# Attention stage of a two-layer block: two of ScalarE's four squares behind the next exponentials, VectorE's query remainder ahead of its wait for GpSimd, two row maxima ahead of x's statistics

## The chip, the cores and the metric

The kernel runs on one core of a Trainium2 chip. The metric is the device time of one launch in microseconds (us). TensorE does the matrix products into PSUM, VectorE (DVE in the rows) and ScalarE (ACT) read PSUM and SBUF, GpSimd (POOL) works from SBUF, and SyncE (SP) issues all DMAs of the stage that the change touches.

## What is computed

The reference has four steps for 32 sequences of 256 tokens with 256 features; the change lies in the first two and in the distances for the third:

```
def _layernorm(x):  m, v = mean(x), var(x);  return (x - m) / sqrt(v + eps)

x = x + tanh(g_xattn[0]) * xattn(_layernorm(x), ctx, ctx, wq, wk, wv, wo)   # 16 heads of 16
x = x + tanh(g_ffn[0])   * ffn(_layernorm(x), ...)
x = x + tanh(g_xattn[1]) * align(ctx, _layernorm(x))    # distances, path, gather
x = x + tanh(g_ffn[1])   * ffn_quantised(_layernorm(x), ...)

def xattn(query, key, value, ...):
    scores = q @ k.T / sqrt(256)                        # per head, 256 x 256
    return (softmax(scores) @ v) @ wo.T
def ffn(x, ...):
    h = bitlinear(x, w_fc) + gate * (x @ v.T @ fast_b.T @ u.T)    # 1024 wide
    r = maximum(h, 0)
    return bitlinear(r * r, w_proj)
```

## The kernel before

`build` calls three phases one after the other: `attention_phase` (line 103; the first two steps and the distances), `alignment_phase` and `last_layer_phase`. Only the first is changed.

`attention_phase` is a software pipeline over the 32 sequences ("batches", `NB`). Each engine runs a hand-written `iteration(i)`, for i from -4 to 33, in which several batches are at different stages: `a` = i+2 (queries and keys are made and split in three bf16 parts), `s` = i+1 (first scores and their row maxima), `i` (second scores, exponentials, values), `z` = i-1 (output projection, first half of the ffn), `y` = i-2 (second half of the ffn, distances), `nx` = i+3 (x's statistics). TensorE runs its iteration as a loop, the others unrolled. The order on each engine is the order of the calls in `iteration`; between engines only semaphores hold things together (`w(name, count)` waits, `.then_inc` counts up). An engine works strictly in its order: what stands behind a waiting instruction waits too.

The pieces that matter here, with their lines:

- **Scores, first pass.** `scores1` (L380) writes the scores of head h into the PSUM tile `s1[h % 2]`; `maxima` on VectorE (L799) reduces it to negative row maxima `nmax`. With two tiles, scores of head h+2 wait for the maxima of head h. After head 15 `max_transpose` (L387) turns `nmax`, and `split_max` (L739, L740) makes two bf16 rows of it, which a DMA puts under the queries.
- **Scores, second pass.** `scores2` (L395) writes `s2[h % 2]`, `exps` on ScalarE (L595) takes the exponentials into `pt[h % 8]`, `values` (L407) multiplies four heads at a time. Scores of head h+2 wait for the exponential of head h; `values(g)` waits for exponentials up to head 4g+3.
- **The ffn's squares.** `fc(z, k)` (L473 to L477), k = 0 to 3, makes 256 of the 1024 columns; `relu` (L625, ScalarE) makes `rl[k % 2]` from it with two instructions and, in the kernel before, the high half of its square at once, `r2h` (L631). GpSimd squares `rl` exactly into the only buffer `r2` (L886), and `low_squares` on VectorE (L768) makes the low half `r2l` from `r2` and `r2h`. GpSimd's next square waits for it. `proj` (L344, L345) uses both halves in the next iteration.
- **The norms.** VectorE collects statistics (`x_stats`, and inside `residual1`, `residual2`; L713), aggregates them (L719), writes the variances `ln_v` (L832) and waits for `ln_rstd`: GpSimd raises them to the power -0.5 (L897, `ln_y`). Then VectorE makes `yn` (`ln3`), `xh2` (`ln2`) and `xhat` (`ln1`), all on L725.
- **The query remainder.** `queries` (L321) fills the bank `B_QUERIES`; `qh_copy` (L574, ScalarE) rounds it to `qp`, `q_remainder` (L749, VectorE) makes `qr` from bank and copy. `turn_xh2` (L315), which transposes `xh2` into the same bank (`B_XH2`; three PSUM tiles `wb` serve 18 uses in turn), waits for `ln2` and for `q_remainder`:

```
def turn_xh2(b):
    w("ln2", b.n + 1)
    w("qh_cp", b.n + 4), w("q_rem", b.n + 4)
```

- **The key remainder** (L745, `kr`) opens VectorE's iteration, in the same way as the query's.

In the rows buffer numbers are left out: `s` is s1 or s2 (L380 writes s1, L395 s2), `pt` the exponentials, `wb` the shared PSUM banks, `xh` is xh2, `x` is x1 or x2, and `r` is r2.

Of the kernel before, what the change touches and what calls it, by code (L numbers as in the profile page):

```python
# [102 lines left out]
def attention_phase(nc, io, scr):  # L103
# [3 lines left out]
    with ExitStack() as ctx:  # L107
# [84 lines left out]
        def unrolled(iteration):  # L192
            for n in range(-4, NB + 2):
                iteration(Batch(n // 2, n % 2))
# [20 lines left out]
        def there(b):  # L215
            return not isinstance(b.n, int) or 0 <= b.n < NB
# [342 lines left out]
        @block.scalar  # L559
        def _(act):  # L560
            def w(s, count, most=NB):
                done(act, e[s] if isinstance(s, str) else s, count, most)

            def xT_copy(b):
                w("xhat_t", b.n + 1), w("q_mm", b.n)
                act.activation(xT[:], B_TURN_X[:], ACT.Copy).then_inc(e["xT_cp"], 1)

            def kh_copy(b):
                w("k_mm", b.n + 1), w("k_out", 16 * b.n, 16 * NB)
                act.activation(kp[:, 0, :, :], B_KEYS[:], ACT.Copy).then_inc(e["kh_cp"], 1)  # L570

            def qh_copy(b):
                w("q_mm", b.n + 1), w("q_out", 16 * b.n, 16 * NB)
                act.activation(qp[:, 0, :, :], B_QUERIES[:], ACT.Copy, scale=1.0 / 16).then_inc(e["qh_cp"], 1)  # L574

            def middle_part(b, rem, r, parts, s):
                w(rem, b.n + 1)
                act.activation(parts[:, 1, :, :], r[:], ACT.Copy).then_inc(e[s], 1)

            def onT_copy(b):  # L580
                w("on_t", b.n + 1), w("wo_mm", b.n)
                act.activation(onT[:], B_TURN_ON[:], ACT.Copy).then_inc(e["onT_cp"], 1)

            def values_copy(b):
                w("v_mm", b.n + 1), w("av_mm", NG * (b.n - 1), NG * NB)
                for t in range(T):
                    last = act.activation(vw[b.p][:, t, :, 0:DH], B_VALUES[:, t, :].rearrange("p (h m) -> p h m", m=DH),
                                          ACT.Copy)
                last.then_inc(e["vw_cp"], 1)

            def exps(b, lo, hi):
                for h in range(lo, hi):
                    w("s2_mm", NH * b.n + h + 1, NH * NB)
                    w("av_mm", NG * b.n + h // HPG - 1, NG * NB)
                    act.activation(pt[h % (2 * HPG)][:], s2[h % 2][:], ACT.Exp).then_inc(e["expd"], 1)  # L595

            def copy_group(b, g):
                w("av_mm", NG * b.n + g + 1, NG * NB)
                w("o_t", 2 * (b.n - 1) + g // 2 + 1, 2 * NB)
                act.activation(osb[:, g, :], oacc[:, g % 2, :], ACT.Copy).then_inc(e["o_cp"], 1)  # L600

            def yT_copy(b):
                w("y_t", b.n + 1), w("ab_mm", b.n)
                act.activation(yT[:], B_TURN_Y[:], ACT.Copy).then_inc(e["yT_cp"], 1)

            def xh2_copy(b):
                w("xh2_t", b.n + 1), w("fc_mm", 4 * b.n, 4 * NB)
                act.activation(x2h[:], B_XH2[:], ACT.Copy).then_inc(e["x2T_cp"], 1)

            def low_copy(b):  # L610
                w("low_mm", b.n + 1), w("fc_mm", 4 * b.n, 4 * NB)
                act.activation(lowt[:], B_LOW[:, 1, :], ACT.Copy).then_inc(e["low_cp"], 1)

            def half_copy(b):
                w("half_t", b.n + 1), w("ab_mm", b.n)
                for t in range(T):
                    rows = slice(32 * t, 32 * t + 32)
                    last = act.activation(hrows[rows, t * P:t * P + P], B_LOW[rows, 0, 0:P], ACT.Copy)
                last.then_inc(e["half_cp"], 1)

            def relu(b, k):
                w("fc_mm", 4 * b.n + k + 1, 4 * NB)
                w("squared", 4 * b.n + k - 1, 4 * NB)
                for j in range(2):
                    last = act.activation(rl[:, k % 2, j, :], B_FC[k][:, j, :], ACT.Relu,  # L625
                                          scale=fscl[:, 2 * k + j:2 * k + j + 1])
                last.then_inc(e["relu"], 1)
                w("relu", 4 * b.n + k + 1, 4 * NB)
                if k == 0:
                    w("pr_mm", b.n)  # L630
                act.activation(r2h[:, 2 * k:2 * k + 2, :], rl[:, k % 2], ACT.Square).then_inc(e["sq_high"], 1)  # L631

            def ctx_squares(b):
                w(c_in[b.p], 16 * (b.half + 1), 16 * NB)
                w("dist", b.n - 1)
                for t in range(T):
                    w("aa_sum", T * b.n + t, T * NB)
                    act.activation(junk[:], cin[b.p][:, t, :], ACT.Square, accum_out=aa[b.p][:, t:t + 1])\
                        .then_inc(e["aa_sum"], 1)

            def distance(b):
                w("ab_mm", b.n + 1), w("d_out", 16 * T * b.n, 16 * T * NB)
                w("aa_sum", T * (b.n + 1), T * NB)
                for t in range(T):
                    last = act.activation(dd[:, t, :], B_PRODUCTS[:, t, :], ACT.Relu, bias=aa[b.p][:, t:t + 1], scale=-2.0)  # L645
                last.then_inc(e["dist"], 1)

            def iteration(i):
                s, a, z, y = i.off(1), i.off(2), i.off(-1), i.off(-2)
                if there(a):  # L650
                    xT_copy(a)
                    kh_copy(a)
                if there(z):
                    onT_copy(z)
                if there(a):
                    middle_part(a, "k_rem", kr, kp, "k_parts_mid")
                if there(z):
                    ctx_squares(z)
                if there(i):
                    exps(i, 0, 4)  # L660
                if there(a):
                    qh_copy(a)
                if there(i):
                    copy_group(i, 0)
                    exps(i, 4, 6)
                if there(s):
                    values_copy(s)
                if there(i):
                    exps(i, 6, 8)
                if there(y):  # L670
                    yT_copy(y)
                if there(z):
                    xh2_copy(z)
                if there(a):
                    middle_part(a, "q_rem", qr, qp, "q_parts_mid")
                if there(y):
                    half_copy(y)
                if there(i):
                    copy_group(i, 1)
                if there(y):  # L680
                    distance(y)
                if there(z):
                    low_copy(z)
                if there(i):
                    exps(i, 8, 10)
                if there(z):
                    relu(z, 0)
                if there(i):
                    exps(i, 10, 12)
                if there(z):  # L690
                    relu(z, 1)
                if there(i):
                    exps(i, 12, 14)
                    copy_group(i, 2)
                    exps(i, 14, 16)
                if there(z):
                    relu(z, 2)
                if there(i):
                    copy_group(i, 3)
                if there(z):  # L700
                    relu(z, 3)
            unrolled(iteration)

        @block.vector
        def _(v):
# [106 lines left out]
            def iteration(i):  # L812
                s, a, nx, z, y = i.off(1), i.off(2), i.off(3), i.off(-1), i.off(-2)
                if there(a):
                    k_remainder(a)
                if there(nx):
                    x_stats(nx)
                if there(s):
                    maxima(s, 0, 4)
                if there(y):  # L820
                    residual2(y)
                if there(s):
# [4 lines left out]
                if slots:  # L827
                    w("halves", y.n)
                    aggregate(slots[0], slots[-1] + 1)
                    c = slice(T * slots[0], T * (slots[-1] + 1))  # L830
                    w("ln_rstd", i.n + 3, NB + 5)
                    v.tensor_scalar(ln_v[:, c], ln_mv[:, c, 1], EPS, None, ALU.add).then_inc(e["ln_var"], 1)  # L832
                    w("ln_rstd", i.n + 4, NB + 5)
                if there(y):
                    ln3(y)
                if there(z):
                    ln2(z)
                if there(a):
                    q_remainder(a)
                if there(nx):  # L840
                    ln1(nx)
                if there(z):
# [1001 lines left out]
```

## Time and profile before

| | |
|---|---|
| median of 3 runs | 1934.49 us (1932.57 to 1935.65) |
| profiled execution | 1930.39 us, its span 1928.6 us |
| TensorE busy, of the span | 1454.7 us (75%) |
| VectorE busy | 1438.4 us (75%) |
| ScalarE busy | 1108.1 us (57%) |
| GpSimd busy | 560.7 us (29%) |

The span is drawn from the first to the last instruction; the time of the run holds about 2 us more. Busy shares are means over three phases. The attention phase ends a little after 1230 us; what the tables say of it is read from windows inside it. A row of the timeline has the start, the duration of the merged group, the engine, the line, the operation, the tiles (written <- read), the count, and in brackets the idle time before it and whom it waited for.

### The profile page before, as it was taken

What the parts mean: (1) busy time and instruction counts of PE and PEld (TensorE: products, weight loads), DVE (VectorE), ACT (ScalarE), POOL (GpSimd) and SP (SyncE); (2) the same over time, 40 slices, a digit from 0 to 9 for tenths busy, and PEclk for the clock granted to TensorE, in tenths of its full rate; (3) what the DMA queues carried; (4) which work ended last, traced back from release to release, by engine and by line L of the source; (5) the groups of instructions that cost most, each with busy time, mean ns of one, the idle gap of its engine ahead of it and who ended that gap; (6) DMA issues with size and microseconds to landing.
All of it is one profiled execution on the core that took longest, in us unless ns stands there. A gap on an engine that the chain in (4) does not pass through costs nothing. (4 is left out here: it accounts for less than half of the span.)

```text
span 1928.6 us, 35799 instructions
## 1 busy us (share of the span) xinstructions
PE 1454.7 (75%) x10821; PEld 1062.1 (55%) x10821; DVE 1438.4 (75%) x4102; ACT 1108.1 (57%) x2374; POOL 560.7 (29%) x1002
## 2 busy tenths in 40 slices
PE   1689999999999999999999997423333001889986
PEld 1367777777777777777777775300000000566664
DVE  7466667666666676666666664299999998999996
ACT  0166666666666666666666665224333300899997
POOL 4112222322222222222222222210000000778786
PEclk9799999999999999999999999755555555899999
DMA  2544444434444344344443421222221001232221
GB/s 74 123 140 111 130 113 140 117 106 133 118 120 121 109 140 119 106 131 118 125 118 109 128 76 39 58 64 61 58 59 28 0 0 49 66 99 91 91 89 45
DMA packets 322936, 179.49 MB, mean 93 GB/s; under 512 B 93793, under 2 KB 318193, under 8 KB 322802
## 3 DMA queue, kind: packets, MB, share of 16 engines
q1 hardware_dynamic: 322802, 178.07, 33.5%
q8 instruction: 40, 0.66, 0.1%
q14 instruction: 94, 0.77, 0.1%
HBM read 122.91 MB, written 50.33 MB: 90 GB/s over the span
## 5 line engine op out<-in xcount | busy, mean ns | idle before, releaser
L799 DVE TENSOR_REDUCE nmax<-s 128x2 f32<-128x512 f32 x512 | 325.1, 682 | 41.1 <-PE s L380 40.0
L595 ACT ACTIVATE pt<-s 128x512 f32<-128x512 f32 x512 | 277.4, 596 | 83.7 <-PE s L395 83.6
L886 POOL TENSOR_TENSOR r<-rl 128x512 f32<-128x512 f32 x128 | 133.3, 1042 | 369.4 <-ACT rl L625 366.8
L380 PE MATMUL s<-kst,qst 96*128 96x256 bf16 x1024 | 163.3, 276 | 18.2 <-DVE nmax L799 12.8
L395 PE MATMUL s<-qst,kst 128*128 128x256 bf16 x1024 | 167.6, 276 | 9.2 <-ACT pt L595 1.4
L1298 PE MATMUL gate<-diag,one 128*128 128x512 f16 x35 | 21.3, 608 | 176.7 <-DVE left L1385 176.7
L625 ACT ACTIVATE rl<-wb,fscl 128x256 f32<-128x256 f32 x256 | 107.4, 473 | 81.1 <-PE wb L477 81.1
L473 PE MATMUL wb<-x2l,wfcT 128*128 128x256 f32 x512 | 143.3, 302 | 0.5 <-ACT dd L645 0.5
L407 PE MATMUL oacc<-pt,vw 128*32 128x256 f32 x2048 | 137.1, 385 | 2.0 <-ACT pt L595 2.0
L344 PE MATMUL wb<-wprT,r2l 128*128 128x256 f32 x512 | 129.3, 292 | 6.9 <-DVE r2l L768 6.9
L474 PE MATMUL wb<-x2h,wfcT 128*128 128x256 f32 x512 | 132.7, 281 | 0.0
L897 POOL TENSOR_TENSOR ln_y<-ln_v,ln_pow 128x6 f32<-128x6 f32 (+2 forms) x37 | 44.6, 1204 | 298.7 <-DVE ln_v L832 298.6
L1408 DVE SCALAR_TENSOR_TENSOR hop<-iota,path,steps 32x256 f32<-32x256 f32 x255 | 120.7, 473 | 12.4 <-DMA steps<-step 3.4
L345 PE MATMUL wb<-wprT,r2h 128*128 128x256 f32 x512 | 123.6, 281 | 0.0
L768 DVE TENSOR_TENSOR r2l<-r,r2h 128x512 fp32r<-128x512 f32 x128 | 88.3, 690 | 45.7 <-POOL r L886 45.7
L395 PEld LDWEIGHTS s<-qst,kst 128*128 128x128 bf16 x1024 | 81.0, 98 | 73.3 <-ACT pt L595 48.6
L380 PEld LDWEIGHTS s<-kst,qst 96*128 96x128 bf16 x1024 | 91.4, 98 | 53.3 <-DVE nmax L799 31.7
L1298 PEld LDWEIGHTS gate<-diag,one 128*128 128x128 f16 x35 | 3.7, 105 | 194.1 <-DVE left L1385 175.5
L344 PEld LDWEIGHTS wb<-wprT,r2l 128*128 128x128 f32 x512 | 97.2, 190 | 8.6 <-DVE r2l L768 7.9
L1372 DVE TENSOR_TENSOR_SCAN rows_r<-best,rows_r,rows_d 128x64 f32<-128x64 f32 x280 | 100.7, 360 | 0.2
L1584 ACT ACTIVATE apart<-iota,mid 128x256 f32<-128x256 f32 x64 | 28.7, 509 | 124.0 <-DVEq L1790 118.9
L473 PEld LDWEIGHTS wb<-x2l,wfcT 128*128 128x128 f32 x512 | 97.0, 189 | 2.0 <-issue 0.6
(266 smaller groups left out, 3963.3 us busy)
## 6 DMA issues: line engine op xcount, KB each, us to landing
kst<-k_parts_dram SPq DMA_DIRECT2D x384, 64.0 KB, 2.7
qst<-q_parts_dram SPq DMA_DIRECT2D x384, 64.0 KB, 2.4
k_parts_dram<-kp SPq DMA_DIRECT2D x32, 384.0 KB, 5.1
q_parts_dram<-qp SPq DMA_DIRECT2D x32, 384.0 KB, 3.1
xin<-in_x_dram SPq DMA_DIRECT2D x32, 256.0 KB, 2.9
cT<-in_ctx_T_dram SPq DMA_DIRECT2D x32, 256.0 KB, 2.7
xres<-in_x_dram SPq DMA_DIRECT2D x32, 256.0 KB, 3.2
cin<-in_ctx_dram SPq DMA_DIRECT2D x32, 256.0 KB, 4.4
```

The source lines that it names most:

```text
L344: pe.matmul(B_PROJ[:, t, :], r2l[:, f, t * P:t * P + P], wprT[:, f, :], start=(f == 0), stop=False)
L345: last = pe.matmul(B_PROJ[:, t, :], r2h[:, f, t * P:t * P + P], wprT[:, f, :], start=False, stop=(f == FT - 1))
L380: last = pe.matmul(s1[h % 2][:, t, :], qst[b.p][0:MAXROW, h, t * P:t * P + P], kst[b.p][0:MAXROW, h, :], start=True, stop=True)
L395: last = pe.matmul(s2[h % 2][:, t, :], kst[b.p][:, h, t * P:t * P + P], qst[b.p][:, h, :], start=True, stop=True)
L407: last = pe.matmul(oacc[HW * j:HW * j + HW, g % 2, :], vw[b.p][:, t, HPG * g + j, :], pt[(HPG * g + j) % (2 * HPG)][:, t, :], start=(t == ...
L473: pe.matmul(B_FC[k][:, j, :], wfcT[:, c, f * P:f * P + P], x2l[:, c, :], start=(c == 0), stop=False)
L474: pe.matmul(B_FC[k][:, j, :], wfcT[:, c, f * P:f * P + P], x2h[:, c, :], start=False, stop=False)
L595: act.activation(pt[h % (2 * HPG)][:], s2[h % 2][:], ACT.Exp).then_inc(e["expd"], 1)
L625: last = act.activation(rl[:, k % 2, j, :], B_FC[k][:, j, :], ACT.Relu, scale=fscl[:, 2 * k + j:2 * k + j + 1])
L799: v.tensor_reduce(nmax[:, T * h:T * h + T], s1[h % 2][:], AX.X, ALU.max, negate=True)\
L886: pool.tensor_tensor(r2[:], rl[:, k % 2], rl[:, k % 2], ALU.mult)\
L1408: ch.link(v.scalar_tensor_tensor(hop[:], iota[:], path[:, i + 1:i + 2], steps[:, i, :], ALU.is_le, ALU.mult, accum_out=path[:, i:i + 1]))
```

## The change

ScalarE: the square leaves `relu` and becomes a function `square` of its own, called for k = 0 after `exps(i, 10, 12)` and for k = 1 after `exps(i, 12, 14)`; for k = 2 and 3 it still follows its `relu`. VectorE: `maxima(s, 0, 2)` is called ahead of `x_stats(nx)`, and `q_remainder(a)` ahead of the wait for `ln_rstd` and thus ahead of `ln3` and `ln2`. No instruction is added or removed.

```
                     last = act.activation(rl[:, k % 2, j, :], B_FC[k][:, j, :], ACT.Relu,
                                           scale=fscl[:, 2 * k + j:2 * k + j + 1])
                 last.then_inc(e["relu"], 1)
+
+            def square(b, k):
                 w("relu", 4 * b.n + k + 1, 4 * NB)
                 if k == 0:
                     w("pr_mm", b.n)
...
                 if there(i):
                     exps(i, 10, 12)
                 if there(z):
+                    square(z, 0)
                     relu(z, 1)
                 if there(i):
                     exps(i, 12, 14)
+                if there(z):
+                    square(z, 1)
+                if there(i):
                     copy_group(i, 2)
                     exps(i, 14, 16)
                 if there(z):
                     relu(z, 2)
+                    square(z, 2)
                 if there(i):
                     copy_group(i, 3)
                 if there(z):
                     relu(z, 3)
+                    square(z, 3)
...
                 if there(a):
                     k_remainder(a)
+                if there(s):
+                    maxima(s, 0, 2)
                 if there(nx):
                     x_stats(nx)
                 if there(s):
-                    maxima(s, 0, 4)
+                    maxima(s, 2, 4)
...
                     w("ln_rstd", i.n + 3, NB + 5)
                     v.tensor_scalar(ln_v[:, c], ln_mv[:, c, 1], EPS, None, ALU.add).then_inc(e["ln_var"], 1)
+                if there(a):
+                    q_remainder(a)
+                if slots:
                     w("ln_rstd", i.n + 4, NB + 5)
                 if there(y):
                     ln3(y)
                 if there(z):
                     ln2(z)
-                if there(a):
-                    q_remainder(a)
                 if there(nx):
                     ln1(nx)
```

On ScalarE, in a steady iteration from the ffn's first quarter to its third, there stood before (`s2_0`, `s2_1` are the two tiles of second scores, `rl` and `r2h` the relu and its square):

```order
L625 ACTIVATE rl<-wb0,fscl 128x256 x2
L631 ACTIVATE r2h<-rl 128x512
L595 ACTIVATE pt2<-s2_0 128x512
L595 ACTIVATE pt3<-s2_1 128x512
L625 ACTIVATE rl<-wb1,fscl 128x256 x2
L631 ACTIVATE r2h<-rl 128x512
L595 ACTIVATE pt4<-s2_0 128x512
L595 ACTIVATE pt5<-s2_1 128x512
L600 ACTIVATE osb<-oacc 128x256
```

and now stands, with the lines of the changed kernel (2 higher from L631 on):

```order
L625 ACTIVATE rl<-wb0,fscl 128x256 x2
L595 ACTIVATE pt2<-s2_0 128x512
L595 ACTIVATE pt3<-s2_1 128x512
L633 ACTIVATE r2h<-rl 128x512
L625 ACTIVATE rl<-wb1,fscl 128x256 x2
L595 ACTIVATE pt4<-s2_0 128x512
L595 ACTIVATE pt5<-s2_1 128x512
L633 ACTIVATE r2h<-rl 128x512
L600 ACTIVATE osb<-oacc 128x256
```

Each square went behind the two exponentials that followed it.

On VectorE, at the start of a steady iteration, there stood before (`xin0` is x's tile for the statistics, `s1_0` and `s1_1` the tiles of first scores):

```order
L745 TENSOR_TENSOR kr<-wb1,kp 128x512
L713 BN_STATS ln_st<-xin0 128x6 x2
L799 TENSOR_REDUCE nmax<-s1_0 128x2
L799 TENSOR_REDUCE nmax<-s1_1 128x2
L799 TENSOR_REDUCE nmax<-s1_0 128x2
```

and now:

```order
L753 TENSOR_TENSOR kr<-wb1,kp 128x512
L807 TENSOR_REDUCE nmax<-s1_0 128x2
L807 TENSOR_REDUCE nmax<-s1_1 128x2
L721 BN_STATS ln_st<-xin0 128x6 x2
L807 TENSOR_REDUCE nmax<-s1_0 128x2
```

The two reductions for heads 0 and 1 went ahead of the two statistics instructions.

On VectorE, around the wait for GpSimd's power (behind `ln_v`), there stood before:

```order
L832 TENSOR_SCALAR ln_v<-ln_mv 128x6
L725 TENSOR_SCALAR yn<-x2,ln_mv,ln_y 128x256 x2
L725 TENSOR_SCALAR xh2<-x1_0,ln_mv,ln_y 128x256 x2
L749 SCALAR_TENSOR_TENSOR qr<-wb2,qp 128x512
L725 TENSOR_SCALAR xhat<-xin0,ln_mv,ln_y 128x256 x2
```

and now:

```order
L842 TENSOR_SCALAR ln_v<-ln_mv 128x6
L757 SCALAR_TENSOR_TENSOR qr<-wb2,qp 128x512
L733 TENSOR_SCALAR yn<-x2,ln_mv,ln_y 128x256 x2
L733 TENSOR_SCALAR xh2<-x1_0,ln_mv,ln_y 128x256 x2
L733 TENSOR_SCALAR xhat<-xin0,ln_mv,ln_y 128x256 x2
```

The query remainder went from behind `xh2` to ahead of `yn` and of the wait that stands in front of it.

## Rows read from the trace of the kernel before

**Rows 1.** Busy time by window, steady attention: us, busy (count) per engine, PEclk, DMA share, GB/s

```profile
180.00:1127.00 947.00, 923.33 (x7372) 718.53 (x7371) 648.63 (x1428) 618.98 (x1381) 257.02 (x379) 1.00 0.43 120
```

**Rows 2.** Timeline of TensorE, first scores of heads 2 and 3, iterations 21 and 29

```profile
818.56 0.27 PE L345 MATMUL wb<-wprT,r2h 128*128 128x256 f32 x1
818.81 0.39 PE L380 MATMUL s<-kst,qst 96*128 96x256 bf16 x2
819.41 0.39 PE L380 MATMUL s<-kst,qst 96*128 96x256 bf16 x2 [0.20 <-DVE nmax L799]
...
1098.97 0.61 PE L380 MATMUL s<-kst,qst 96*128 96x256 bf16 x4
```

**Rows 3.** Timeline of VectorE, iteration 21, its start

```profile
817.42 0.75 DVE L713 BATCH_NORM_STATS2 ln_st<-xin 128x6 f32<-128x256 f32 x2
818.08 2.47 DVE L799 TENSOR_REDUCE nmax<-s 128x2 f32<-128x512 f32 x4
```

**Rows 4.** Timeline of TensorE, turns of yn and xh2 and the values behind them, iterations 21 and 29

```profile
830.45 0.60 PE L315 MATMUL wb<-ident,yn 128*128 128x128 f32 x4
831.41 0.63 PE L315 MATMUL wb<-ident,xh 128*128 128x128 f32 x4 [0.36 <-DVE qr L749]
831.97 1.07 PE L407 MATMUL oacc<-pt,vw 128*32 128x256 f32 x16
...
1110.24 0.60 PE L315 MATMUL wb<-ident,yn 128*128 128x128 f32 x4
...
1111.36 1.07 PE L407 MATMUL oacc<-pt,vw 128*32 128x256 f32 x16
```

**Rows 5.** Timeline of VectorE, iteration 21, norms and query remainder

```profile
829.28 0.73 DVE L725 TENSOR_SCALAR yn<-x,ln_mv,ln_y 128x256 f32<-128x256 f32 x2 [1.45 <-POOL ln_y L897]
829.93 0.73 DVE L725 TENSOR_SCALAR xh<-x,ln_mv,ln_y 128x256 f32<-128x256 f32 x2
830.58 0.69 DVE L749 SCALAR_TENSOR_TENSOR qr<-wb,qp 128x512 f32<-128x512 f32 x1
```

**Rows 6.** Timeline of GpSimd, the power; one small step in iterations 21 and 32

```profile
827.92 1.33 POOL L897 TENSOR_TENSOR ln_y<-ln_v,ln_pow 128x6 f32<-128x6 f32 x1 [8.51 <-DVE ln_v L832]
...
831.05 0.20 POOL L905 TENSOR_TENSOR hrest<-half,hpb 128x2 f32<-128x2 f32 x1
...
1204.89 0.20 POOL L905 TENSOR_TENSOR hrest<-half,hpb 128x2 f32<-128x2 f32 x1
```

**Rows 7.** Timeline of ScalarE, iteration 21: the query copy, exponentials of heads 6 and 7

```profile
826.50 0.60 ACT L574 ACTIVATE qp<-wb 128x512 bf16<-128x512 f32 x1 [2.59 <-PE wb L321]
...
830.43 1.08 ACT L595 ACTIVATE pt<-s 128x512 f32<-128x512 f32 x2
```

**Rows 8.** Timeline of TensorE, iterations 20 and 21: second scores of heads 12 to 15, and behind

```profile
805.90 0.88 PE L395 MATMUL s<-qst,kst 128*128 128x256 bf16 x4
...
840.90 0.88 PE L395 MATMUL s<-qst,kst 128*128 128x256 bf16 x4
...
843.26 0.88 PE L395 MATMUL s<-qst,kst 128*128 128x256 bf16 x4
843.98 0.60 PE L380 MATMUL s<-kst,qst 96*128 96x256 bf16 x4
...
846.70 0.28 PE L387 MATMUL wb<-ident,nmax 128*32 128x128 f32 x1
```

**Rows 9.** Timeline of ScalarE, iteration 21: squares and exponentials of heads 10 to 13

```profile
839.73 0.63 ACT L631 ACTIVATE r2h<-rl 128x512 fp32r<-128x512 f32 x1
840.27 1.06 ACT L595 ACTIVATE pt<-s 128x512 f32<-128x512 f32 x2
841.22 0.84 ACT L625 ACTIVATE rl<-wb,fscl 128x256 f32<-128x256 f32 x2
...
842.63 1.06 ACT L595 ACTIVATE pt<-s 128x512 f32<-128x512 f32 x2
```

**Rows 10.** Timeline of VectorE, iteration 21: maxima of heads 14 and 15

```profile
844.40 1.29 DVE L799 TENSOR_REDUCE nmax<-s 128x2 f32<-128x512 f32 x2 [0.48 <-PE s L380]
```

More of the change, by code:

```diff
@@ L627, in relu, with square @@
                 last.then_inc(e["relu"], 1)
+            def square(b, k):
                 w("relu", 4 * b.n + k + 1, 4 * NB)
@@ L690, in iteration @@
                 if there(z):
+                    square(z, 0)
                     relu(z, 1)
@@ L693, in iteration @@
                     exps(i, 12, 14)
+                if there(z):
+                    square(z, 1)
+                if there(i):
                     copy_group(i, 2)
@@ L697, in iteration @@
                     relu(z, 2)
+                    square(z, 2)
                 if there(i):
@@ L701, in iteration @@
                     relu(z, 3)
+                    square(z, 3)
             unrolled(iteration)
@@ L815, in iteration @@
                     k_remainder(a)
+                if there(s):
+                    maxima(s, 0, 2)
                 if there(nx):
@@ L818, in iteration @@
                 if there(s):
-                    maxima(s, 0, 4)
+                    maxima(s, 2, 4)
                 if there(y):
@@ L832, in iteration @@
                     v.tensor_scalar(ln_v[:, c], ln_mv[:, c, 1], EPS, None, ALU.add).then_inc(e["ln_var"], 1)
+                if there(a):
+                    q_remainder(a)
+                if slots:
                     w("ln_rstd", i.n + 4, NB + 5)
@@ L837, in iteration @@
                     ln2(z)
-                if there(a):
-                    q_remainder(a)
                 if there(nx):
```

## The prediction

> **What bounds the kernel now.** I read the slices and the busy time by window first. In the steady stretch of the attention phase TensorE is busy 923.33 of 947 us at a granted clock of 1.00, which is its level of 2.4 GHz, while VectorE and ScalarE are busy two thirds of it [rows 1]. TensorE sets the pace there, so an edit on another engine is worth what it takes from TensorE's waits. Then I read the waits and TensorE's timeline of one period. The period is 35.00 us (the same group of second scores starts at 805.90 and 840.90, [rows 8]) and repeats unchanged from iteration 2 to 28. All rows here are from iteration 21 (813.4 to 848.4 us) or from iteration 29, which lacks x's statistics. The chain that ended last lies in the third phase and says nothing about this one. Three places in the period have TensorE waiting for work that the change moves:
>
> - *First scores of heads 2 and 3.* The last projection matmul starts at 818.56, and its kind comes 0.12 apart, so the scores could start near 818.68. They start at 818.81, and the second pair only at 819.41: four matmuls take from 818.81 to 819.80, 0.99 us, where iteration 29 shows 0.61 [rows 2]. The wait is for the maxima, which VectorE starts at 818.08, behind x's statistics [rows 3]. In iteration 29, without these statistics, it is gone.
> - *The turn of xh2.* It starts at 831.41 for want of the query remainder, 830.58 + 0.69 = 831.27 [rows 4, 5].
> - *Second scores of heads 12 to 15.* Both groups of four take 0.88 us [rows 8] where an undisturbed one takes 0.61 (the same count and columns, [rows 2]): their second pair waits for an exponential.
>
> **The change part by part.**
>
> *A, squares behind exponentials.* Before, a square starts at 839.73 and the exponentials of heads 10, 11 at 840.27: it holds them back by 0.54 us [rows 9]. Now they start at 839.73, then the square, and the relu for k = 1 starts at 841.22 as before, since the same work stands ahead of it. It lasts until the next instruction at 841.22 + 0.87 = 842.09 (0.84 and the step to the next), and the exponentials of heads 12, 13 start there, not at 842.63: 0.54 earlier. Scores of head 15 wait for the exponential of head 13. It ended at 842.63 + 1.06 = 843.69 and the following first scores started at 843.98 [rows 8, 9]; now it ends at 843.15 and these start at about 843.45. I take 0.53 us per iteration. The first group's stall (0.27 and the start) lies inside this: TensorE comes earlier to the second group and meets the rest there, about 0.3 us of waiting that stays. What the later squares cost: the copy of the values' third group keeps its time, since the second square still stands ahead of it. VectorE's low half for k = 0 waits for a square that ends near 841.3, for k = 1 near 843.7, about 0.9 us later than before. VectorE works in order and the maxima of heads 14, 15 stand behind; they would start near 844.35 and end near 845.64, against 844.40 and 845.69 before [rows 10]. The transpose of the maxima, at 846.70 before [rows 8], comes at 846.17. So 0.5 us of cover is left; if it were gone, each further microsecond would be TensorE's. GpSimd's second square waits for the low half of k = 0 (near 842.05) and for the relu (842.06): nothing. It applies in iterations 1 to 31, in which exponentials and squares meet: 31 x 0.53 = 16.4 us.
>
> *B, the query remainder under the power.* VectorE sits 1.45 us in front of yn for the power, which GpSimd runs from 827.92 to 829.25 [rows 5, 6]. The remainder needs ScalarE's copy, done at 827.10 [rows 7]; it starts at about 827.83 and ends at 828.5, inside this wait. Its cost is nothing; uncovered it would be 0.60 (its step to the next) in front of yn and xh2. xh2 is ready at 829.93 + 0.73 = 830.66 and TensorE, four matmuls behind 830.45 (0.60 for the group, the last of them 0.27 long and 0.11 apart, so 0.44 to the next), comes for it at 830.89. So the stall of 0.52 goes. What is late next: the values of heads 4 to 7 wait for the exponential of head 7, which ends at 830.43 + 1.08 = 831.51 [rows 7]. They start at 831.56, not at 831.97: 0.41 us. Iteration 29 has a power that is 0.3 shorter and no xhat, and shows this limit: from the turn of yn to the values 1.12 us, against 1.52 here [rows 4], a gain of 0.40. I take 0.41 and iterations 1 to 28: 11.5 us. GpSimd's second part of the queries and their DMA keep their place behind ScalarE's middle part, which does not move.
>
> *C, two maxima ahead of x's statistics.* The maxima of heads 0, 1 start at 817.42 and end at 818.10 and 818.70; TensorE wants them at 818.68 and 818.91, so both parts of the stall go: 0.13 + 0.38 = 0.51 at most, I take 0.49. The statistics and heads 2, 3 then end at about 820.6 as before, and VectorE still waits for TensorE behind them. Nobody waits for the statistics before the aggregate. Iterations 2 to 28: 27 x 0.49 = 13.2 us. In iterations before that the maxima stand in one unbroken row on VectorE, whose end doesn't move: nothing.
>
> No DMA is moved and no wait on SyncE's queue gains a later event than before; its transfers are issued from events that move forward with TensorE.
>
> *Where a page and the sum differ.* TensorE's idle time by the window row is 947 - 923.33 = 23.7 us in 27 periods, 0.87 us each [rows 1], and A, B and C together claim 1.43. The two can both hold because a row's duration covers a matmul's way through the array, so that short waits between matmuls hide inside durations; I count from start to start. The Trainium skill says just this in "Perfetto Trace Analysis", section Identifying the Most-Contended Engine: matmul busy share is no good measure of the room left, the share of weight loads is better. Here weight loads are busy 718.53 of 947 us, 76% [rows 1], which leaves far more room than 0.87 us. By the busy rows alone the sum would be that of the second rival.
>
> *Sum.* 16.4 + 11.5 + 13.2 = 41.1 us. The profiled execution has 1930.39 (span 1928.6); 1930.39 - 41.1 = 1889.3. The median of the runs shown lies 4.1 us above the profiled one, so the forecast against it is **1893.4 us**, 2.1% below 1934.49. The later phases keep their time.
>
> **Rivals.**
>
> 1. *The remainder slows the power.* GpSimd's power and VectorE's remainder now run together, and if one held the other up by the remainder's 0.69 us, yn would end at 830.70 and xh2 at 831.35, and TensorE would be at 831.49, 0.08 later than before. B would turn from 11.5 saved to 2 lost: 1893.4 + 13.7 = 1907. Against: a small GpSimd step right beside the remainder took 0.20 us, and 0.20 too where VectorE was idle [rows 6]. For: the power itself never ran beside it. Chance 0.11.
> 2. *Only visible idle time comes back.* The bracketed idle is 0.20 for C and 0.36 for B [rows 2, 4] and none for A: 0.56 x 28 = 16 us, so 1918. Against: the 0.88 and 0.61 us groups and iteration 29. Chance 0.06.
> 3. *Slower: the squares hold up VectorE.* The two low halves now wait for later squares with four reductions queued behind. From the point where the maxima of head 15 end after 846.1 TensorE waits at their transpose, and from about 2 us of delay, 1.43 + 0.5, the change loses. With 3 us it is about 1 us in each of 31 iterations: 1934.5 + 31 = 1966. For: the margin is small beside this chain of four engines. Against: every link is reckoned from rows, with 0.5 left. Chance 0.04.
> 4. *Nothing.* The moved work is on the path nowhere, because another wait takes each place (the relu of k = 3, a DMA): 1934. The order of the instructions does move as the change says. Chance 0.03.
>
> **How the numbers follow.** The forecast has 0.76. Its bounds: per iteration from 0.40 + 0.32 + 0.38 = 1.10 to 0.54 + 0.41 + 0.51 = 1.46, and up to 4 us at the pipeline's ends and between runs: 1887 to 1904. To hold 8 in 10 with some of rival 1, the range is 1886 to 1909. A measurement here tells a change of about 0.2% (4 us) from none; faster by more are the forecast and rivals 1 and 2, 0.93; the same 0.03; slower 0.04.
>
> **What would show it.** Right: a period of about 33.6 us instead of 35.0; no wait of the xh2 turn for qr; first scores of heads 2, 3 in one group of 0.61; the second scores of heads 12, 13 at 0.61 and those of 14, 15 still stretched; the power still 1.33 us; the values of heads 4 to 7 directly behind the exponential of head 7. Wrong: the transpose of the maxima waiting for VectorE, a power near 2 us, or a new wait of TensorE that isn't in the list of before.

## The result, and the profile after

| | before | changed |
|---|---|---|
| median (4 runs each, same chip) | 1933.53 us (1931.96 to 1935.65) | 1883.97 us (1883.32 to 1887.86) |
| profiled execution | 1930.39 us | 1887.86 us, its span 1886.1 us |
| ratio, 95% interval | | 0.9752 (0.974 to 0.9763) |
| steady period of the attention phase | 35.00 us | 33.40 us |

Faster by 2.5%, where 2.1% were forecast: 1883.97 against 1893.4, and 2 us below the lower end of the range. Two later sets of runs of the changed kernel gave medians of 1887.63 and 1886.46 us, ratios 0.9764 (0.9747 to 0.978) and 0.9761 (0.9748 to 0.9774). Both medians lie just inside the range, so the first is on the favourable side of what the kernel does. But the gain from median to median was 49.6 us at first and 46.9 and 46.3 later, against 41.1 forecast: most of the miss stays.

Busy time by window of the changed kernel's steady stretch (columns as in [rows 1]):

```profile
180.00:1080.00 900.00, 894.57 (x7329) 722.50 (x7331) 646.40 (x1423) 606.51 (x1374) 253.04 (x378) 1.00 0.45 126
```

The granted clock is 1.00 as before. TensorE's rows leave 5.4 of 900 us idle, 0.20 us a period, against 0.87: the rows show 0.67 us of a gain that is 1.60 by the starts. Counting from start to start was right.

The timeline of TensorE in the changed kernel, the three places in order of the iteration (the period that begins near 815 us):

```profile
820.59 0.61 PE L380 MATMUL s<-kst,qst 96*128 96x256 bf16 x4
821.04 0.60 PE L395 MATMUL s<-qst,kst 128*128 128x256 bf16 x4
...
831.86 0.60 PE L315 MATMUL wb<-ident,yn 128*128 128x128 f32 x4
832.30 0.60 PE L315 MATMUL wb<-ident,xh 128*128 128x128 f32 x4
833.06 1.07 PE L407 MATMUL oacc<-pt,vw 128*32 128x256 f32 x16 [0.16 <-ACT pt L595]
```

The first scores of heads 2 and 3 are one group of 0.61 us, where there were 0.99 in two [rows 2]. The turn of xh2 waits for nothing, but the values of heads 4 to 7 now wait for an exponential: from the turn of yn to these values 1.20 us, against 1.52 [rows 4].

And one period earlier, its last third:

```profile
806.35 0.61 PE L395 MATMUL s<-qst,kst 128*128 128x256 bf16 x4
...
808.41 0.61 PE L395 MATMUL s<-qst,kst 128*128 128x256 bf16 x4
...
810.40 0.63 PE L395 MATMUL s<-qst,kst 128*128 128x256 bf16 x4
810.87 0.60 PE L380 MATMUL s<-kst,qst 96*128 96x256 bf16 x4
...
813.60 0.28 PE L387 MATMUL wb<-ident,nmax 128*32 128x128 f32 x1
```

Both groups that took 0.88 [rows 8] take 0.61 and 0.63. The stretched rest in the second group, which the forecast left, isn't there. From the group for heads 10, 11 to the transpose of the maxima it is 7.25 us; before it was 8.04 (838.66 to 846.70, the first of these from the same timeline).

The timeline of ScalarE there:

```profile
806.54 0.84 ACT L625 ACTIVATE rl<-wb,fscl 128x256 f32<-128x256 f32 x2 [1.09 <-PE wb L477]
807.27 1.09 ACT L595 ACTIVATE pt<-s 128x512 f32<-128x512 f32 x2
808.23 0.65 ACT L633 ACTIVATE r2h<-rl 128x512 fp32r<-128x512 f32 x1
808.75 0.86 ACT L625 ACTIVATE rl<-wb,fscl 128x256 f32<-128x256 f32 x2
809.46 1.12 ACT L595 ACTIVATE pt<-s 128x512 f32<-128x512 f32 x2
```

The exponentials start 0.73 and 0.71 us after the relus in front of them. The square started 0.87 after its relu before: the forecast carried that 0.87 over to the exponentials. An exponential starts before the relus have ended (807.27 against 806.54 + 0.84 = 807.38), a square that follows its relus only after their end (839.73 against 838.86 + 0.84 = 839.70). From the kernel before, the relus ahead of the first square in [rows 9]:

```profile
838.86 0.84 ACT L625 ACTIVATE rl<-wb,fscl 128x256 f32<-128x256 f32 x2 [1.08 <-PE wb L477]
```

From relu to relu it is 2.21 us, where it was 2.36 (838.86 to 841.22). The square is not slow to start by itself: behind the two exponentials it starts 0.96 us after their start, and the relu that stood there before started after 0.95 (840.27 to 841.22, [rows 9]).

On VectorE and GpSimd:

```profile
811.20 0.69 DVE L776 TENSOR_TENSOR r2l<-r,r2h 128x512 fp32r<-128x512 f32 x1 [0.35 <-ACT r2h L633]
811.81 1.28 DVE L807 TENSOR_REDUCE nmax<-s 128x2 f32<-128x512 f32 x2
813.92 0.28 DVE L747 CAST nsp<-wb 32x128 bf16<-32x128 f32 x1 [0.83 <-PE wb L387]
```

```profile
829.19 0.69 DVE L757 SCALAR_TENSOR_TENSOR qr<-wb,qp 128x512 f32<-128x512 f32 x1
```

```profile
829.33 1.33 POOL L908 TENSOR_TENSOR ln_y<-ln_v,ln_pow 128x6 f32<-128x6 f32 x1 [8.01 <-DVE ln_v L842]
```

The low half does wait for the late square, and the last maxima end at 813.09, 0.51 us ahead of their transpose on TensorE: the cover of rival 3 was 0.5 as reckoned. The power takes 1.33 us with the remainder beside it, as before [rows 6]: rival 1 is out.

### The profile page after: what moved, and what is told of

The parts are those of the page before. It is cut to its first block and busy times, and to the rows that moved or that the text cites. A ratio compares the mean times of both kernels' runs of the same rounds, so it can differ in the third digit from the quotient of the medians.

```text
span 1886.1 us, 35769 instructions
## 1 busy us (share of the span) xinstructions
PE 1433.6 (76%) x10790; PEld 1074.4 (57%) x10821; DVE 1436.9 (76%) x4102; ACT 1097.6 (58%) x2374; POOL 558.5 (30%) x1002
## 5 line engine op out<-in xcount | busy, mean ns | idle before, releaser
L595 ACT ACTIVATE pt<-s 128x512 f32<-128x512 f32 x512 | 281.4, 612 | 70.0 <-PE s L395 70.0
L380 PE MATMUL s<-kst,qst 96*128 96x256 bf16 x1024 | 158.9, 275 | 11.8 <-DVE nmax L807 7.3
L395 PE MATMUL s<-qst,kst 128*128 128x256 bf16 x1024 | 157.3, 275 | 1.1 <-ACT pt L595 0.8
L345 PEld LDWEIGHTS wb<-wprT,r2h 128*128 128x128 f32 x512 | 99.2, 194 | 0.0
```

The source lines that it names most:

```text
L345: last = pe.matmul(B_PROJ[:, t, :], r2h[:, f, t * P:t * P + P], wprT[:, f, :], start=False, stop=(f == FT - 1))
L380: last = pe.matmul(s1[h % 2][:, t, :], qst[b.p][0:MAXROW, h, t * P:t * P + P], kst[b.p][0:MAXROW, h, :], start=True, stop=True)
L395: last = pe.matmul(s2[h % 2][:, t, :], kst[b.p][:, h, t * P:t * P + P], qst[b.p][:, h, :], start=True, stop=True)
```

## The experiments

Theory D: the surplus is in part A. A square that follows its relu directly reads what the relu has just written and waits for its end; an exponential doesn't. Each square moved frees this wait, some 0.14 us, besides its own 0.54. Rival R: A is worth the 0.53 of the forecast, and the rest arises from the parts together. A second question is where the spread of several us between executions comes from, since the sum was shifted by 4.1 us for it. Theory T: it lies in TensorE's clock in the last iterations.

**Each part alone.** The edits are the hunks of the change: ScalarE's alone, the one with `q_remainder` alone, the one with `maxima` alone.

> Only part A (the squares of k = 0 and 1 behind the next exponentials). Theory D (a square reads what the relu just wrote and must wait for its end, an exponential need not; each moved square frees 0.54 us and about 0.14 of that wait besides): period 34.21 us instead of 35.00, relu to exponential 0.73 us instead of relu to square 0.87, both groups of second scores of heads 12 to 15 at 0.61 to 0.63; time lower by 31 x 0.79 = 24 us. Rival R (A is worth the 0.53 of the forecast and the rest of the surplus comes from the parts together): period 34.47, the second group still stretched, 16 us.

> Only part B (query remainder ahead of the wait for the power). If the stage in the changed kernel tells its worth (turn of yn to values of heads 4 to 7 1.52 to 1.20 us): period 34.68, time lower by 28 x 0.32 = 9 us. By the forecast's 0.41: period 34.59, 11.5 us. The power stays at 1.33 us in both.

> Only part C (two maxima ahead of x's statistics). Both theories: period 34.49 us, time lower by 27 x 0.51 = 14 us; if parts interact (a sum larger than its parts) the three single gains per period add to clearly less than 1.60 us.

| | period | less than 35.00 by | median (runs) | ratio, 95% interval |
|---|---|---|---|---|
| A alone | 34.19 us | 0.81 | 1908.46 (4) | 0.9868 (0.9851 to 0.9884) |
| B alone | 34.68 us | 0.32 | 1926.36 (5) | 0.9965 (0.9951 to 0.9979) |
| C alone | 34.50 us | 0.50 | 1919.29 (4) | 0.9923 (0.9906 to 0.994) |
| all three | 33.40 us | 1.60 | see above | |

Kernel before in these runs: 1934.49 us. The single gains add to 1.63, all three together give 1.60: the parts are independent to 0.03 us, and R is out. A is worth 0.81 and not 0.53; C is what was forecast; B is worth 0.32 and not 0.41. TensorE and ScalarE in the kernel with B alone and in the changed kernel show the same rest, here from B alone:

```profile
822.21 0.60 PE L315 MATMUL wb<-ident,yn 128*128 128x128 f32 x4
822.65 0.60 PE L315 MATMUL wb<-ident,xh 128*128 128x128 f32 x4
823.41 1.07 PE L407 MATMUL oacc<-pt,vw 128*32 128x256 f32 x16 [0.16 <-ACT pt L595]
```

In the changed kernel the exponentials of heads 6 and 7:

```profile
831.84 1.09 ACT L595 ACTIVATE pt<-s 128x512 f32<-128x512 f32 x2
```

They end at 832.93 and the values start at 833.06: 0.13 us from the end of what is waited for to the matmul, where I had put 0.05.

The 0.05 came from iteration 29 of the kernel before, and it is right for that iteration. TensorE's iteration is a loop only from 4 to 27 (`run`); the iterations ahead of it and behind it are written out. The changed kernel shows both. In iteration 28, outside the loop, ScalarE, then TensorE's turns, then its weight loads (PEld):

```profile
1032.28 1.09 ACT L595 ACTIVATE pt<-s 128x512 f32<-128x512 f32 x2
1032.30 0.60 PE L315 MATMUL wb<-ident,yn 128*128 128x128 f32 x4
1033.42 0.59 PEld L407 LDWEIGHTS oacc<-pt,vw 128*32 128x32 f32 x16 [0.32 <-ACT pt L595]
```

The exponentials end at 1033.37 and the values' first weight load starts at 1033.42, 0.05 later, although it has waited. From the turn of yn it is 1.12 us, as in iteration 29 of before. The single instructions of the trace show what differs: outside the loop the weight load carries the wait for the exponential itself; inside it a register instruction of 0.03 us carries it, 0.08 ahead of the weight load. So it is in every trace of a kernel with B: 0.12 us to the weight load in the loop's iterations, 0.05 outside. With B alone the period is 34.61 outside the loop and 34.68 inside.

**One square at a time.** The first edit keeps the square of k = 1 behind its relu, the second that of k = 0:

```
                 if there(z):
                     square(z, 0)
                     relu(z, 1)
+                    square(z, 1)
                 if there(i):
                     exps(i, 12, 14)
-                if there(z):
-                    square(z, 1)
```

```
                 if there(z):
                     relu(z, 0)
+                    square(z, 0)
                 if there(i):
                     exps(i, 10, 12)
                 if there(z):
-                    square(z, 0)
                     relu(z, 1)
```

Both without B and C.

> Only the square of k = 0 moved; that of k = 1 stays behind its relu. The exponentials of heads 10, 11 come early, then square and relu as before, so by the forecast's reckoning the relu of k = 1 starts when it did and the second scores of head 15 too: period 35.00 us, nothing gained. Theory D (a square that follows its relu directly waits about 0.14 us for its end): relu to relu is 2.21 us instead of 2.36, the exponentials of heads 12, 13 come 0.15 earlier, period 34.85.

> Only the square of k = 1 moved. The stall of the group for heads 12, 13 stays (0.88), that of heads 14, 15 goes: 0.27 and 0.1 in front of it, period near 34.6 us by both theories. They differ in the step from the relu of k = 1 to the exponential: 0.87 us by the forecast, 0.73 by theory D.

The first has a period of 34.86 us. Theory D said 34.85, the forecast's reckoning 35.00. ScalarE in it:

```profile
837.32 0.84 ACT L625 ACTIVATE rl<-wb,fscl 128x256 f32<-128x256 f32 x2 [1.08 <-PE wb L477]
838.05 1.09 ACT L595 ACTIVATE pt<-s 128x512 f32<-128x512 f32 x2
839.00 0.65 ACT L633 ACTIVATE r2h<-rl 128x512 fp32r<-128x512 f32 x1
839.52 0.86 ACT L625 ACTIVATE rl<-wb,fscl 128x256 f32<-128x256 f32 x2
840.41 0.63 ACT L633 ACTIVATE r2h<-rl 128x512 fp32r<-128x512 f32 x1
```

One trace has both steps: relu to exponential 0.73 us, relu to square 0.89, and relu to relu 2.20 with the same three instructions in it that took 2.36 in the other order. The median was 1931.21 us (8 runs), 0.9992 (0.9982 to 1.0002) of before: by time alone this 0.14 us a period, 4 us in all, wouldn't be seen; the period shows it.

The second has 34.62 us, a gain of 0.38, near 34.6 as both theories said, with 0.88 in the first group and 0.61 in the second, and a step of 0.71 from the relu of k = 1 to the exponential. Its ratio is 0.9945 (0.9925 to 0.9966), from 2 runs. So the squares are worth 0.14 and 0.38 one by one and 0.81 together. The first square's 0.54 reaches TensorE only if the second lets it: moved alone, the exponentials of heads 12, 13 hold the second group (TensorE waits 0.35 in front of it and it takes 0.88):

```profile
841.58 0.88 PE L395 MATMUL s<-qst,kst 128*128 128x256 bf16 x4 [0.35 <-ACT pt L595]
```

What counts is not a sum of two terms but the later of two waits.

**The spread between executions.**

> The changed kernel unchanged, for the spread of its executions. Theory T (the place of a profiled execution in its kernel's spread differs by some us with TensorE's clock in the last four iterations, whose waits are long): period 33.40 again to 0.02 us, iterations 31 to 33 between 87 and 93 us in sum, shorter where the granted clock is higher, and the time follows them. Rival: the steady period varies between executions and carries the spread.

> The kernel before unchanged, for a second trace of it. Theory T (the profiled execution of before had a high granted clock in its last iterations and so stood below its median): the last three periods add to more than the 87.5 us of that one, the time is nearer 1934 than 1930, the steady period is 35.00 again.

In both kernels the steady periods repeat to a few hundredths (35.00 and 33.40 in every trace, the latter 33.33 outside TensorE's loop; the kernel before has 35.25 twice, in iterations 10 and 26, in both of its traces). What differs is the phase's end. Iterations 31 to 33, from the half norms' transpose of iteration 30 to that of 33, as windows of the four traces: kernel before (profiled 1930.39 us), kernel before again (1934.73), changed kernel (1887.86), changed kernel again (1883.92):

```profile
1144.98:1232.52 87.54, 65.28 (x486) 50.46 (x483) 36.35 (x82) 42.25 (x97) 19.59 (x36) 0.95 0.12 31
```

```profile
1144.97:1236.48 91.51, 69.30 (x486) 53.43 (x483) 36.34 (x82) 42.24 (x97) 19.55 (x36) 0.88 0.11 30
```

```profile
1099.62:1191.34 91.72, 70.18 (x486) 54.35 (x483) 36.28 (x82) 41.70 (x97) 19.56 (x36) 0.86 0.11 30
```

```profile
1098.81:1187.12 88.31, 66.74 (x486) 52.01 (x483) 36.30 (x82) 41.69 (x97) 19.59 (x36) 0.90 0.12 31
```

The counts are the same; the length follows the granted clock (0.95 and 0.90 against 0.88 and 0.86), and the differences of 4.0 and 3.4 us are nearly those of the times, 4.3 and 3.9. They stand in TensorE's own busy time, 65.28 against 69.30 and 66.74 against 70.18 for the same matmuls, while the other engines' hardly differs. Theory T holds. Here TensorE waits for other engines and falls to its level of 1.2 GHz in stretches that differ from one execution to the next; in the changed kernel's profiled execution such a stretch shows by the step of the matmuls:

```profile
1149.03 0.28 PE L344 MATMUL wb<-wprT,r2l 128*128 128x256 f32 x1
...
1150.34 0.41 PE L344 MATMUL wb<-wprT,r2l 128*128 128x256 f32 x1
1150.56 0.41 PE L345 MATMUL wb<-wprT,r2h 128*128 128x256 f32 x1
```

They come 0.22 us apart instead of 0.12. The profiled execution of before had an end with a high clock and stood low in its spread, that of the changed kernel one with a low clock and stood high.

**Going on from there.** After the change TensorE still stood at two places: the key projection waited about 0.2 us for the relu of k = 3 of the iteration before (they share a PSUM tile), and the values of heads 4 to 7 for the exponential of head 7. The first edit, on TensorE and VectorE:

```
                 if there(a):
                     turn_x(a)
-                    keys(a)
-                if there(z):
-                    turn_on(z)
                 if there(s):
                     scores1(s, 0, 2)
+                if there(a):
+                    keys(a)
+                if there(z):
+                    turn_on(z)
...
-                if there(a):
-                    k_remainder(a)
                 if there(s):
                     maxima(s, 0, 2)
+                if there(a):
+                    k_remainder(a)
```

> The changed kernel, with TensorE's first scores of heads 0, 1 ahead of the key projection and VectorE's maxima 0, 1 ahead of the key remainder. The key projection waits about 0.2 us for the relu of k = 3 (same PSUM tile); the scores would cover it. If nothing else waits for the keys: period 33.40 - 0.2 = 33.2 us, 6 us less than the changed kernel. Rival: the key remainder comes 0.3 later on VectorE, ScalarE's and GpSimd's key parts follow, and the maxima of heads 2, 3 behind it hold the scores of heads 4, 5: period 33.4 or more.

The period is 33.06 us, 0.34 less, and the ratio to before 0.9739 (0.9722 to 0.9756) at a median of 1881.07 us (5 runs). I had expected 0.2. TensorE in it:

```profile
812.41 0.60 PE L315 MATMUL wb<-ident,xhat 128*128 128x128 f32 x4
812.85 0.60 PE L380 MATMUL s<-kst,qst 96*128 96x256 bf16 x4
813.28 1.89 PE L321 MATMUL wb<-cT,wkT 128*128 128x256 f32 x8
815.01 0.60 PE L315 MATMUL wb<-ident,on 128*128 128x128 f32 x4
```

in the changed kernel:

```profile
815.35 0.60 PE L315 MATMUL wb<-ident,xhat 128*128 128x128 f32 x4
816.01 1.99 PE L321 MATMUL wb<-cT,wkT 128*128 128x256 f32 x8
817.84 0.60 PE L315 MATMUL wb<-ident,on 128*128 128x128 f32 x4
```

The wait of 0.22 is gone, and 0.10 within the projection besides: it takes 1.73 us from its start to the next group where it took 1.83 behind the wait. By the single matmuls the 0.10 lies between the first and the second (0.32 us against 0.22). Why was not tried apart.

The second edit exchanges TensorE's calls for heads 6 and 7, alone and with the first:

```
                 if there(s):
                     values_proj(s)
-                    scores1(s, 6, 8)
                 if there(i):
                     scores2(i, 6, 8)
+                if there(s):
+                    scores1(s, 6, 8)
```

> The changed kernel with only the exchange of scores for heads 6, 7: period 33.40 - 0.1 = 33.30 us if the exponential of head 6 starts 0.1 earlier, 33.40 if not; 3 us at most.

> Keys behind the first scores as in the run before, and TensorE's second scores of heads 6, 7 ahead of the first scores of heads 6, 7. What B left over is the wait of the values of heads 4 to 7 for the exponential of head 7 (0.32 us a period). The exponential of head 6 starts at the end of ScalarE's values copy, 0.1 later than an instruction that waits for nothing could, because its scores are just ready; 0.44 us earlier scores give this 0.1 back: period 33.06 - 0.1 = 32.96 us, 3 us less. If the values copy is the limit to the last, 33.06.

> The changed kernel unchanged, on the same chip as the two others: period 33.40 us, time 1883 to 1889 us, following the granted clock in the last four iterations.

| five runs each, same chip | period | median | ratio to before, 95% interval |
|---|---|---|---|
| changed kernel | 33.40 us | 1886.46 us | 0.9761 (0.9748 to 0.9774) |
| heads 6, 7 exchanged | 33.26 us | 1882.81 us | 0.9749 (0.9736 to 0.9763) |
| both edits | 32.95 us | 1878.60 us | 0.9720 (0.9707 to 0.9733) |

The kernel before had 1932.8 us (9 runs). The exchange gives 0.14 of the period alone (0.1 was expected) and 0.11 behind the other edit; by time alone it can't be told from the changed kernel, as the intervals overlap. The exponentials of heads 6, 7 start 0.54 us behind ScalarE's copy of the values, where it was 0.66: that is the 0.1. The version with both beats the changed kernel: the intervals of the two ratios don't touch.

## Why the prediction was wrong

The direction and the three places were as forecast, and the rivals fell. The range was missed by 2 us, by one term, and in part by a first set of runs on the fast side.

- **A, the term that was mis-sized.** The step that failed is "Now they start at 839.73, then the square, and the relu for k = 1 starts at 841.22 as before, since the same work stands ahead of it". The same instructions did stand there, but not the same waits. The exponentials start 0.73 us behind the relu, not 0.87, and the relu of k = 1 starts 2.21 behind the first, not 2.36. A gives 0.79 to 0.81 a period, not 0.53; over 31 periods 8 us more. In all the exponentials of heads 12, 13 come 0.85 us earlier behind the first relu (2.92 us, before 3.77), 0.54 of the moved square and 0.15 and 0.16 of its waits. That is enough for TensorE's two groups to be whole again, so "about 0.3 us of waiting that stays" fell too. The term's upper bound, 0.54, left no room for this.
- **B.** The limit was named rightly, the exponential of head 7; the release took 0.13 us and not 0.05 in the 24 iterations of TensorE's loop. The gain there is 0.32 and not 0.41, over 24 periods 2.2 us less; outside the loop it is 0.40 and more, as forecast. Iteration 29, which I took for proof of 0.40, is written out behind the loop: the step was read from code that differs from the steady one.
- **C.** 0.50 to 0.51 against 0.49, as forecast.
- **The sum.** By the corrected terms 31 x 0.80 + 24 x 0.32 + 4 x 0.41 + 27 x 0.51 = 47.9 us, of which 47.1 up to the last transpose of the maxima, in iteration 30. Measured there are 46.2 (1158.74 against 1112.55) in the first traces of both kernels and 46.95 in the second ones. The three parts together give 1.60 and not 1.63, 0.8 less in 27 periods, and the two periods of 35.25 that are gone give 0.5 back, which makes 46.8. What is left is within the 0.8 by which the first iterations differ between two traces of the changed kernel. Behind it the clock at the end took 4.2 back in the profiled execution: 41.2 at iteration 33, and 42.5 at the end of the run. That this is so near the forecast 41.1 is chance: the second traces of the same two kernels are 50.8 us apart (1934.73 and 1883.92).
- **The shift to the median.** "The median of the runs shown lies 4.1 us above the profiled one, so the forecast against it is 1893.4 us." This is the same as 1934.49 - 41.1, and a gain is rightly taken from a median: the profiled execution stood low, with a granted clock of 0.95 at its end, where the second trace had 0.88 and 4.3 us more. Up to 2 us of the 4.1 were chance of a small sample: in later sets before's median was 1934.49, 1932.3 and 1932.8. Without the shift the forecast, 1889.3, would have been nearer, by luck. As a ratio, 41.1 of 1933 would have said 0.9787, outside all three intervals: the term A is the larger part of the miss.
- **The cover.** VectorE's last maxima ended 0.51 us before they were wanted (0.5 forecast), GpSimd's power stayed at 1.33 us. No wait appeared that wasn't in the list, but for that of the values.
- **The idle time by the rows** saw 0.67 us of 1.60. TensorE was busy 923.33 of 947 us by its rows, 97.5%, and still 1.60 of 35.00 us could be taken out without taking any matmul away. The Trainium skill says in "Perfetto Trace Analysis", Identifying the Most-Contended Engine, that the matmul busy share is not a good measure of how close the engine is to its limit; these numbers agree.

## What to carry to other kernels

When an instruction moves out from behind the one it depends on, count the step between the two as two things, the work and the wait for the end of the producer, and take the step of an independent pair from another row. Judge two moves on the same chain together: the later of two waits decides, so that 0.14 and 0.38 us can be 0.81. Take a step that a term rests on from an iteration that runs the same code: one in the loop for the loop, not one that is written out behind it. Before a profiled execution is set against a median, look where the executions differ.

## What was not expected of the hardware

- On ScalarE, a square of the tile that two relus (128x256 each) had just written started 0.87 to 0.89 us after the first relu's start, an exponential of another tile 0.71 to 0.73: the first starts 0.03 after the relus' end each time, the second 0.10 to 0.15 before it. The dependence, which the kernel keeps by a wait for the relu's semaphore, costs about 0.15 us. What it would cost without the semaphore was not tried.
- From the end of an exponential to the start of the matmul that waited for it, 0.13 us inside TensorE's loop, where a register instruction carries the wait, and 0.05 outside, where the weight load carries it.
- The same projection of 8 matmuls took 1.83 us to the next group when it had waited in front, and 1.73 when it had not.
- Three iterations with long waits at the phase's end carried nearly all of the spread of 4 us between executions, by the granted clock (0.86 to 0.95), while 27 steady periods repeated to a few hundredths of a us. The extra 0.24 us in iterations 10 and 26 of the kernel before stays with A or C alone and is gone (0.06 at most) in every kernel that has B; it was not looked into.
